# Three softmax attentions on one Trainium2 core: the second half of the exponential cut by strips of keys, the shifts of the second pair of strips issued behind the next scores, and half of the key-major products issued ahead of the maxima's transposes

## The reference, cut to what matters

```python
scores = jnp.einsum('bhqd,bhkd->bhqk', qh, kh) * scale          # L0, a2: 120 keys; a1: 256 keys
attn = jax.nn.softmax(scores, axis=-1)
# a1 only, after the softmax: a = a * (1 - mask), so the sum runs over all keys, the product over the allowed ones
out = jnp.einsum('bhqk,bhkd->bhqd', attn, vh)
```

## Time and profile before

| what | us |
|---|---|
| runs of the kernel before, median (lowest to highest of 3) | 1125.64 (1125.37 to 1126.42) |
| the profiled execution | 1123.37 |
| its span | 1121.7 |
| TensorE busy | 1044.7 (93%) |
| VectorE busy | 534.0 (48%) |
| ScalarE busy | 457.6 (41%) |
| GpSimd busy | 269.7 (24%) |

### The profile page before, as it was taken

How to read it: one execution, slowest core, us unless ns; L and a number is a source line. 1 busy time by engine, 2 the same in 40 slices (tenths; PEclk the granted TensorE clock), 3 DMA queues, 4 the chain that set the end, 5 groups by cost and what they waited for, 6 DMA issues and landing times.

```text
span 1121.7 us, 20739 instructions
## 1 busy us (share of the span) xinstructions
PE 1044.7 (93%) x8669; PEld 721.2 (64%) x8679; DVE 534.0 (48%) x1245; ACT 457.6 (41%) x651; POOL 269.7 (24%) x409
## 2 busy tenths in 40 slices
PE   7999965998999999999999999999999999999997
PEld 4555633554455655565766565666677658999996
DVE  5567688886247778753323323676321233300000
ACT  6767644675445555544123225555312221122220
POOL 3023201010113333324022100556410102222211
PEclk9999996999999999999999999999999999999999
DMA  8600000000060000000000020000710317755410
GB/s 255 84 2 1 2 1 0 1 1 1 1 148 3 2 2 2 2 2 1 1 0 1 1 75 20 2 2 2 225 38 2 111 38 272 268 169 192 172 55 1
DMA packets 55358, 60.55 MB, mean 54 GB/s; under 512 B 23603, under 2 KB 47071, under 8 KB 55266
## 3 DMA queue, kind: packets, MB, share of 16 engines
q1 hardware_dynamic: 52322, 52.93, 15.8%
q0 software_dynamic: 2944, 6.30, 1.8%
HBM read 54.76 MB, written 7.21 MB: 55 GB/s over the span
## 4 chain that ended last, share of the span: by engine, by line
PE 77%; DVE 13%; ACT 5%; issue 2%; DMA 1%; SPq 1%; POOL 0%; DVEq 0%; POOLq 0%
PE ps L1635 15%; PE ps L1854 10%; DVE small L782 9%; PE ps L1996 7%; PE ps L2009 7%; PE ps L1773 5%; PE ps L1552 4%; PE ps L1586 3%; PE ps L1533 3%; PE ps L1775 2%; PE ps L1929 2%; PE ps L1543 2%; PE ps L1672 2%; PE ps L1530 2%; PE ps L1468 2%
## 5 line engine op out<-in xcount | busy, mean ns | idle before, releaser
L782 DVE TENSOR_REDUCE small<-ps 128x16 f32<-128x1920 f32 (+1 forms) x64 | 142.3, 2224 | 68.2 <-PE ps L1533 48.0
L1209 ACT ACTIVATE r_a<-ps 120x1024 f32<-120x1024 f32 (+1 forms) x128 | 124.1, 1021 | 28.9 <-PE ps L1568 28.6
L1635 PE MATMUL ps<-r_w,r_k 128*128 128x256 f32 x512 | 113.2, 381 | 2.5 <-ACT r_k L1369 2.5
L1854 PE MATMUL ps<-r_a,r_w 128*128 128x512 f32 x256 | 112.1, 594 | 3.1 <-ACT r_a L1287 3.1
L1635 PEld LDWEIGHTS ps<-r_w,r_k 128*128 128x128 f32 x512 | 96.4, 190 | 18.6 <-issue 4.4
L1586 PE MATMUL ps<-r_a,onesf 128*32 128x256 f32 (+1 forms) x768 | 90.5, 385 | 8.2 <-ACT r_a L1209 8.1
L1996 PE MATMUL ps<-r_a,w_block 128*128 128x128 f32 x736 | 86.4, 275 | 1.0 <-ACT r_a L1430 1.0
L1996 PEld LDWEIGHTS ps<-r_a,w_block 128*128 128x128 f32 x736 | 85.6, 192 | 2.5 <-ACT r_a L1430 1.0
L1854 PEld LDWEIGHTS ps<-r_a,r_w 128*128 128x128 f32 x256 | 48.2, 190 | 60.2 <-issue 56.0
L1369 ACT ACTIVATE r_k<-ps,pvec 128x512 f32<-128x512 f32 x64 | 44.0, 687 | 100.6 <-PE ps L1854 100.6
L2009 PE MATMUL ps<-w_all,r_a 128*128 x368 | 83.2, 379 | 0.2 <-issue 0.2
(11 more groups left out here) (264 smaller groups left out, 1720.2 us busy)
## 6 DMA issues: line engine op xcount, KB each, us to landing
w_block<-in_L_ffn_W SPq DMA_DIRECT2D x23, 1024.0 KB
w_all<-in_L_ffn_W SPq DMA_DIRECT2D x8, 1024.0 KB, 9.4
r_w<-in_L_xattn_a_li_w SPq DMA_DIRECT2D x4, 1024.0 KB, 7.2
x_rows<-x_all SPq DMA_DIRECT2D x4, 512.0 KB, 3.0
x_rows<-r_a SPq DMA_DIRECT2D x4, 512.0 KB, 3.0
x_all<-in_x SPq DMA_DIRECT2D x3, 512.0 KB, 5.5
y_all<-in_L_ffn_w_gate SPq DMA_DIRECT2D x1, 1024.0 KB, 8.8
y_all<-in_L_ffn_w_up SPq DMA_DIRECT2D x1, 1024.0 KB, 11.3
```

Of the source, the lines that this page charges most:

```text
L782: step(dve.tensor_reduce(nm.rearrange("p (j s) -> p j s", j=4), src, AX.X, ALU.max, negate=True))
L1209: act.activation(PT[0:nk, 2 * x:2 * x + 2, :], bank(n % 2, 2 * x, 2)[0:nk], ACT.Exp, scale=scale).then_inc(sem["exp_done"], 1)
L1635: ins_ = pe.matmul(o[:, t // 2, (t % 2) * D:(t % 2 + 1) * D], src[:, c, t * P:(t + 1) * P], w[:, c, :], start=(c == 0), stop=(c == chunks ...
L1854: ins_ = pe.matmul(o, LI[a]["li2"][:, c, m * P:(m + 1) * P], FT3[:, c, :], start=(c == 0), stop=(c == KC - 1))
```

## The change

Three things are moved. `exponentials` keeps one activation of 1024 columns for strips 0 and 1, and makes two of 512 columns for strips 2 and 3, x = 0 and x = 1; `exp_done` counts three per unit. `shifts(n)` is cut by pairs of strips: strips 0 and 1 stay in place, strips 2 and 3 come one round later behind `scores(n+1)`. `key_scores` is cut by x: x = 0 comes ahead of `max_transposes(n)`, waiting for a new semaphore `max_read` that VectorE's reduction sets, x = 1 stays behind it. The sums and products are put in an order that uses the parts of the exponential as they come, and in a1 each masked block has its own count of `pm_ready`. Nothing is added or dropped in the sums that are computed.

```diff
                 def causal(n, h):
-                    pool.wait_ge(sem["exp_done"], 2 * n + h + 1)
                     for x in range(2):
+                        pool.wait_ge(sem["exp_done"], 3 * n + 1 + (x + 1 if h == 1 else 0))
...
-                    ins_.then_inc(sem["pm_ready"], 1)
+                        ins_.then_inc(sem["pm_ready"], 1)
...
-                    step(dve.tensor_reduce(nm.rearrange("p (j s) -> p j s", j=4), src, AX.X, ALU.max, negate=True))
+                    dve.tensor_reduce(nm.rearrange("p (j s) -> p j s", j=4), src, AX.X, ALU.max, negate=True).then_inc(sem["max_read"], 1)
+                    dve.wait_ge(sem["max_read"], n + 1)
...
+                    act.wait_ge(sem["z_done0"], 2 * n + 2)
+                    act.activation(PT[0:nk, 0:2, :], bank(n % 2, 0, 2)[0:nk], ACT.Exp, scale=scale).then_inc(sem["exp_done"], 1)
+                    act.wait_ge(sem["z_done1"], 2 * n + 2)
                     for x in range(2):
-
-                        act.wait_ge(sem[f"z_done{x}"], 2 * n + 2)
-                        act.activation(PT[0:nk, 2 * x:2 * x + 2, :], bank(n % 2, 2 * x, 2)[0:nk], ACT.Exp, scale=scale
+                        act.activation(PT[0:nk, 2:4, S * x:S * (x + 1)], bank(n % 2, 2, 2)[0:nk, :, S * x:S * (x + 1)], ACT.Exp, scale=scale
                                        ).then_inc(sem["exp_done"], 1)
...
+                def causal_values(n):
+
+                    masks = 4 * (n - FIRST["a1"])
+                    pe.wait_ge(sem["exp_done"], 3 * n + 1)
+                    for x in range(2):
+                        for j in (0, 1):
+                            sum_of(n, j, x)
+                    pe.wait_ge(sem["exp_done"], 3 * n + 2)
+                    for j in (2, 3):
+                        sum_of(n, j, 0)
+                    pe.wait_ge(sem["pm_ready"], masks + 2)
+                    for x, q0 in ((0, P), (0, 0), (1, 0)):
+                        for j in (0, 1):
+                            causal_of(n, j, x, q0)
+                    pe.wait_ge(sem["pm_ready"], masks + 3)
+                    for q0 in (P, 0):
+                        for j in (2, 3):
+                            causal_of(n, j, 0, q0)
+                    pe.wait_ge(sem["exp_done"], 3 * n + 3)
+                    for j in (2, 3):
+                        sum_of(n, j, 1)
+                    pe.wait_ge(sem["pm_ready"], masks + 4)
+                    for j in (2, 3):
+                        ins_ = causal_of(n, j, 1, 0)
+                    ins_.then_inc(sem["pv_done"], 1)
...
                         if n0 < n < n1:
                             scores(n)
+                        if n > n0:
+                            shifts(n - 1, 1)
                         if n == n1:
                             pe.wait_ge(sem["os_ready"], n1 - 1)
                             following()
                         if n > n0:
-                            sums(n - 1)
-                            weighted(n - 1)
+                            if a == "a1":
+                                causal_values(n - 1)
+                            else:
+                                sums_and_values(n - 1)
                         if n < n1:
+                            key_scores(n, 0)
                             max_transposes(n)
-                            key_scores(n)
-                            shifts(n)
+                            key_scores(n, 1)
+                            shifts(n, 0)
```

More of the change, by code:

```diff
@@ L1544, in max_transposes, with key_scores, shifts @@
                     ins_.then_inc(sem["maxT_done"], 1)
-                def key_scores(n):
+                def key_scores(n, x):
                     nk = nkeys(n)
[L1550 to L1555, removed]
+                    pe.wait_ge(sem["max_read"], n + 1)
+                    for j in range(4):
+                        pe.matmul(bank(n % 2, j)[0:nk, column(None, x)], keys(n, j, x), queries(n, j, x), start=(x == 0), stop=False,
+                                  tile_position=(32 * j, 0))
+                def shifts(n, h):
                     a = UNIT_OF[n][0]
@@ L1559, in shifts @@
                     pe.wait_ge(sem["maxT_ready"], n + 1)
-                    if n == TOTAL_AT:
+                    if n == TOTAL_AT and h == 0:
                         pe.wait_ge(sem["wsum_ready"], 3)
@@ L1564, in shifts @@
                                   ).then_inc(sem["wtot_done"], 1)
[L1565 to L1572, removed]
+                    for x in range(2):
+                        for j in (2 * h, 2 * h + 1):
+                            ins_ = pe.matmul(bank(n % 2, j)[0:nk, column(None, x)],
+                                             sel[32 * j:32 * j + 32, 0 if a == "a1" else x, 0:nk],
+                                             maxT[32 * j:32 * j + 32, :], start=False, stop=(x == 1), tile_position=(32 * j, 0))
+                            if x == 1:
+                                ins_.then_inc(sem[f"z_done{h}"], 1)
@@ L1574, in weights_of, with sum_of @@
                 def weights_of(n, j, x):
                     return PT[0:nkeys(n), j, S * x:S * (x + 1)]
-                def sums(n):
+                def sum_of(n, j, x):
                     a = UNIT_OF[n][0]
[L1579 to L1587, removed]
@@ L1589, in weighted @@
[L1589 to L1605 removed]
+                    ones = half_ones[0:KV, x, :] if a == "L0" else onesf[0:nkeys(n), 0:32]
@@ new lines, in weighted @@
+                def weighted(n, j, x):
+                    a = UNIT_OF[n][0]
+                    at = S * x if a == "a2" else 0
+                    return pe.matmul(bank(n % 2, 0)[32 * j:32 * j + 32, at:at + S], values(n, j, x), weights_of(n, j, x),
+                                     start=(a == "a2" or x == 0), stop=(a == "a2" or x == 1), tile_position=(0, 32 * j))
+                def causal_values(n):
+                    masks = 4 * (n - FIRST["a1"])
+                    pe.wait_ge(sem["exp_done"], 3 * n + 1)
+                    for x in range(2):
+                        for j in (0, 1):
[18 more added lines that the diff above has]
+                    ins_.then_inc(sem["pv_done"], 1)
@@ new lines, in sums_and_values @@
+                def sums_and_values(n):
+                    pe.wait_ge(sem["exp_done"], 3 * n + 1)
+                    for x in range(2):
+                        for j in (0, 1):
+                            sum_of(n, j, x)
+                    pe.wait_ge(sem["exp_done"], 3 * n + 2)
+                    for j in (2, 3):
+                        sum_of(n, j, 0)
+                    for j in (0, 1):
+                        weighted(n, j, 0)
+                    for j in (2, 3):
+                        weighted(n, j, 0)
+                    for j in (0, 1):
+                        weighted(n, j, 1)
+                    pe.wait_ge(sem["exp_done"], 3 * n + 3)
+                    for j in (2, 3):
+                        sum_of(n, j, 1)
+                    for j in (2, 3):
+                        ins_ = weighted(n, j, 1)
```

23 lines of the change are left out of this document (9 added, 14 removed).

## The result

The changed kernel takes a median of 1143.35 us (1141.88 to 1146.43 in 4 runs), the kernel before 1125.78 us on the same chip (1125.37 to 1126.42 in 4 runs). The ratio is 1.0155, with a 95% interval from 1.0132 to 1.0178: slower by 17.6 us.

What follows compares the result with a forecast made beforehand. TensorE and ScalarE were taken to bound L0, VectorE's reduction a1, scores waiting for `out_copy` a2. Terms of -1.6 (L0), +5.6 (a1) and +9.0 (a2) sum to +13.0, from 1125.64 to 1138.6 us; range 1127 to 1143.5.

Steps and rivals of the forecast that it cites:

- the likeliest case: Whole program: the forecast as summed, 1138.6 us, spanning 1132 to 1143, chance 0.70.
- The group ahead of the transposes: TensorE, between products and transposes: the moved key-major scores cost 0.64 us a unit, or 0.69 behind the reduction.
- Passes only: Rival: the group ahead of the transposes costs only its two passes a strip, 0.43 us; 1126.7 us, chance 0.10.
- the group would run in waiting time: Rival, called faster: the group runs wholly in TensorE's waiting time before the transposes; 1115.6 us, chance 0.12.
- L0: Attention stage L0: period 5.53 instead of 5.64 us, 15 intervals, -1.6 us.
- a1: Attention stage a1: period 5.77 us, between reduction path 5.75 and TensorE path 5.81; +0.18 in 31 intervals, +5.6 us.
- a2: Attention stage a2: period 6.54 against 5.93 us, +0.60 in 15 intervals, +9.0 us.
- Strict order of matmuls: Rival in L0: strips can't pass one another, so second shifts wait for all scores; +2.3 us, 1140.9, chance 0.08.
- Edges: First and last units of the stages: added group hidden in a1's idle time, last products behind long projections; 0 us.

Runs made afterwards that it cites:

- ks_only: The kernel before with only the x = 0 half of the key-major scores moved ahead of the transposes; 1140.11 us, ratio 1.011.
- shifts_back: The changed kernel with the second pair's shifts back directly behind the first pair's, ahead of the next scores; 1133.99 us, ratio 1.0065.
- ks_twice: The changed kernel computing the key-major group ahead of the transposes two times, the second overwriting the first; 1171.59 us in a single run.
- tail_order: The kernel before with exponential cut, out_copy ahead of max_copy in a1 and a2 too, and all sums before products in each stage's last unit; 1118.79 us, single run.
- tail_a2: tail_order with the x = 0 half of the key-major scores ahead of the transposes in a2 alone; 1118.43 us, ratio 0.9931 against the kernel before.
- ks_back: The changed kernel with both halves of the key-major scores behind the transposes again; 1124.78 us, ratio 0.9986 against the kernel before.
- shifts_only: The kernel before with only the second pair's shifts moved behind the next scores; 1135.47 us, ratio 1.0076.
- exp_only: The kernel before with only the exponential cut and the order of sums and products that goes with it; 1124.47 us, ratio 0.9977.

## Why the prediction was right

**The total: right by its mechanism, and in the range with little to spare.** The median of 1143.35 lies 4.75 us above the forecast of 1138.6, just above the 1132 to 1143 of the likeliest case and 0.15 below the upper end of the range. Two of the four runs lie above that end, so that the median came below it is partly luck. What carried the forecast is the price of the group, and the paths in each stage, which the traces bear out as follows.

**The group ahead of the transposes: right, with its size.** 0.64 us behind the products in all three stages, as taken from the 0.71 of the earlier trace rows. Passes only (0.43) is refuted by the rows of after, where the transposes start 0.64 behind the group (417.62 and 418.26), and by the periods of ks_only. That the group would run in waiting time is refuted by ks_only too, where it is the only edit and every stage became slower.

**L0: right mechanism, mis-sized term.** Forecast 5.53, measured 5.60. The term is the quarter's start at 2.40, which rests on 0.92 from start to start; late shifts made it 0.99, and the rest of the chain followed (products' end 5.04 for 4.96, group and transposes as worked out). In the sum, 15 intervals gave -0.45 us in place of -1.6.

**a1: the wrong one of two right paths.** The reduction ended at 5.05 (5.06 in the working) and TensorE's products at 5.26 (5.24). I had 5.75 by the one and 5.81 by the other and took 5.77, nearer to the mean; the later of two paths decides, and it measured 5.83. shifts_back, which takes the TensorE path back, shows the other at 5.75. The term was +5.6 and came to +6.7: 31 x 0.235 = 7.3, less 0.6 because the first interval is 0.33 shorter and not longer (6.60 for 6.93, see the edges).

**a2: right.** 6.53 for 6.54: scores' end, shifts, quarters at 3.39 (3.41 in the working), products' end 5.96 (5.97). The experiments split the +0.60. The group gives 0.22 by the reduction's path as long as the products end early; with late shifts TensorE's path, at 6.53, is the later one, and gives 0.38 more. The late shifts alone give 0.39 with whole halves and nothing with the cut exponential. So the two losses don't add; each stage has one slack, and the edits share it. The total of a2 is +8.2 and not 9.0, since the kernel before has more beside its median interval (90.18 against 15 x 5.93 = 88.95, and 98.40 against 97.95 after): its first a2 interval is 7.04, that of after 6.93, again by the edges.

**Strict order of matmuls: refuted.** In L0 of after, passes of the scores (L1536) start at 83.95, ahead of shifts (L1570) at 84.14 that stand before them in the program, on other strips. The quarter starts at 2.47, and this rival had 2.55. The Trainium skill's rule (TensorE: Matmul & The Clock Gate, The mechanism) that matmuls start and end in program order doesn't hold here across strips of the array. It did not come out as the rival said, but the late shifts weren't free either: 0.07 us by ScalarE.

**Edges: right for the group in a1 and a2, too small elsewhere.** I had 0. The group stands ahead of the first unit's transposes too, and there it puts 0.74 us between the end of the reduction and the transposes:

```profile
33.63 2.16 DVE L782 TENSOR_REDUCE small<-ps 128x16 f32<-128x1920 f32 x1 [0.37 <-PE ps L1533]
...
36.95 0.38 PE L1543 MATMUL ps<-ident,max_rows 128*128 128x128 f32 x2
```
```profile
33.56 2.16 DVE L782 TENSOR_REDUCE small<-ps 128x16 f32<-128x1920 f32 x1 [0.37 <-PE ps L1536]
...
36.98 0.71 PE L1555 MATMUL ps<-r_v,r_k 32*120 32x256 f32 x8
...
37.62 0.44 PE L1546 MATMUL ps<-ident,max_rows 128*128 128x128 f32 x2
```

In L0, before and then after, that is 1.16 and 1.90. It is 1.90 in ks_only and shifts_back as well, 2.33 in ks_twice, and 1.16 or 1.17 in all kernels whose L0 has no group ahead. So the +0.67 before L0 is the group's 0.74, behind a reduction that ended 0.07 sooner (it ends anywhere from 35.6 to 36.8 in the twelve kernels, in no order that follows the edits). It is not hidden: ScalarE's first exponential starts 2.94 behind the reduction before and 3.37 after.

In a1 it is hidden, as I had written, and in a2 too. The transposes of the first unit come 0.74 later behind the reduction (5.20 for 4.46 in a1, 5.38 for 4.64 in a2), but the first exponential starts 7.67 and 7.84 behind it in both kernels. So the later transposes lengthen the stretch ahead of them and shorten the first interval behind them, and time moves from one row of the table to the next without being lost.

The stretch from a1 to a2 grew by 1.11 us. 0.66 of it is the order of the last a1 unit's sums and products (tail_order). I had written that they stand behind long projections, which is so, but nothing hides them there: whatever they take comes on top. The other 0.45 is the 0.74 of the first a2 unit's transposes, less 0.27 by which the last a1 unit's sums start sooner (8.51 behind its transposes for 8.78), to within 0.02. Counted to the first a2 exponential the edge cost 0.4, and not 1.1.

The sum was +13.0 and the medians give +17.6. Of the 4.6 between them, 1.8 are L0 with the start, 1.1 is a1, -0.8 is a2, 1.1 and 0.15 are the stretch to a2 and the rest, and 1.1 is in the stretch from L0 to a1. Of this last one about 0.4 is again the first unit's transposes (0.74, less 0.32 at the last L0 unit). The other 0.7 I can't place; tail_order and tail_a2, whose code is the same there, differ by 1.3 (198.05 and 199.31), so it can be the clock.

## What to carry to other kernels

Work that is moved ahead of a waiting instruction isn't free because "the engine waits there": count from the event that the moved work itself must wait for, add what a group of another layout costs beside its passes, and compare with the wait that was there (0.69 against 0.47 here). Where several edits draw on one slack, work out each path to the next unit's start with all edits in, and take the latest, not a mean and not a sum of single effects. The same wait is often had more cheaply: here two ScalarE instructions in the other order gave 0.31 us in each a2 unit, where three larger edits cost 0.60. An order that follows the arrival of data costs time where all of it is there already (0.66 us in the last a1 unit).

## What the runs showed of the hardware

- Two activations in a row start 0.92 us apart after 1024 columns when the second one's semaphore has come before the first begins, and 0.99 when it comes during the first, even 0.21 us before the second starts (after, ks_back and shifts_only against shifts_back). I had expected any signal ahead of the end to be soon enough.
- A group of 8 passes in a 32-row layout between two of other layouts takes 0.64 us on TensorE (after); doubling it adds 0.43 (ks_twice), so 0.21 are paid once for the group.
- 40 passes on four strips, with nothing to wait for, take 1.67 us when the program goes through the strips in turn and 2.33 when the last eight are all for two of them. Strips do pass one another, but not far enough ahead to make the order indifferent.
- TensorE's clock in the stretch behind L0, where TensorE was busy 22 of 40 us, was at 1.2 GHz for 16.8 us in one execution and 23.2 in another, over nearly the same work. Over the whole stretch from L0 to a1, the twelve profiled executions go from 195.3 us with 17.1 us at that level to 201.9 us with 30.7. That moves single executions by some us, as much as an edit here, and 10 runs of exp_only go from 1120.4 to 1128.1.
